# Fire attention's bias stage: the Relu of a round is taken ahead of the copies of that round's queries and keys

## The chip, the cores and the metric

The kernel runs on one core of a Trainium2 chip. Its engines work side by side, each through its own list of instructions in order: TensorE (PE, with its weight loads shown apart as PEld), VectorE (DVE), ScalarE (ACT), GpSimd (POOL) and SyncE (SP), which here only issues DMAs. They wait for one another through semaphores. The metric is the device time of one execution in microseconds (us), the median of several; lower is better.

## The reference, cut to what matters

The program is a chain of layers on a residual of 2048 tokens by 128 channels, held as 8 batches of 256 tokens. The change touches one layer, attention with a Fire bias, 16 heads of 8 channels:

```
rel  = log(|c * (i - j)| + 1);  pos_norm = log(|c * max(i, threshold)| + 1) + 1e-6
nd   = rel / pos_norm                              # [256, 256]
h    = relu(nd[..., None] * w1 + b1)               # [256, 256, 32]
bias = einsum('tsw,wh->hts', h, w2) + b2           # [16, 256, 256], -inf above the diagonal
att  = softmax(q @ k.T * scale + bias);  y = (att @ v) @ Wproj + bproj
```

The bias doesn't depend on the batch. It is computed once, and q, k and v once for each of the 8 batches.

## The kernel before, in words

All layers run one after the other, each in blocks of code that end in a barrier of all engines. Ahead of Fire attention run two mixtures of experts, a recurrence and a six-layer local transformer; behind it a second local transformer. Fire attention has three blocks. The first loads and prepares `rel` and `pn` (the distances and their reciprocal norms). The second, the bias stage, is the one that is changed. The third computes the scores, the softmax and the output for each batch; it is called the score stage below.

The bias stage has 8 rounds. Round r does two unrelated things: it computes the bias for 32 key positions, and the queries, keys and values of batch r. Its steps, by engine:

- TensorE `project(r)`: four matmuls for queries and keys (the line that the profile calls L1474), then four for values (L1478). Then `biases(r)` (L1488): it waits for the round's Relu (`hd_`) and runs 32 small matmuls in rounds 0 to 3, and 16 in rounds 4 to 7, where half of the keys lie above the diagonal.
- VectorE: `distances(r + 1)` (L1422, eight products into `nd`), then `take_values(r)` (L1435), then `take_bias(r)` (L1428), which waits for the matmuls of `biases(r)`. `distances(0)` stands ahead of the loop. `distances(r)` waits until the Relu of round r - 2 has read its half of `nd`.
- ScalarE: `take_queries(r)` copies the queries (L1457) and the keys (L1461) out of PSUM once `project(r)` has made them; `hidden(r)` (L1452) is one Relu over 128 x 2048 elements, from `nd` to `hb`. It waits for `distances(r)` and for the matmuls of `biases(r - 2)`, which read the same half of `hb`.
- GpSimd: `spread_keys(r)` (L1500) waits for the copy of the keys; then `forget_future(r)` (L1507) waits for `take_bias(r)`.

`nd`, `hb`, `kT` and the PSUM banks of each step are double, by r % 2. Nothing but these lists of instructions and the waits sets the order.

Of the kernel before, what the change touches and what calls it, by code (L numbers as in the profile page):

```python
# [1315 lines left out]
def fire_attention_phase(nc, res, d, M, XN):  # L1316
# [8 lines left out]
    with ExitStack() as ctx:  # L1325
# [43 lines left out]
        with nc.Block() as block:  # L1369
            @block.sync  # L1370
            def _(sp):
                for dst, src in ((sc[:, 0:2], d["fa_sc"].to_broadcast([P, 2])), (rel[:, :], d["c_rel"]), (pn[:, :], d["c_pos"]),
                                 (wb[:, :], d["fa_wb"]), (wqkv[:, :], d["fa_wqkv"]), (bqk[:, :], d["fa_bqk"]),
                                 (bv[:, :], d["fa_bv"].to_broadcast([P, P])), (b2[:, :], d["fa_b2"].to_broadcast([P, NH])),
                                 (hmask[:, :], d["c_hmask"]), (wp[:, :], d["fa_wp"])):
                    sp.dma_start(dst, src).then_inc(ld, 16)
                sp.wait_ge(zd, 1)
                for g in range(4):
                    sp.dma_start(w2[g * BW:(g + 1) * BW, g * NH:(g + 1) * NH], d["fa_w2"]).then_inc(ld, 16)
                sp.wait_ge(ld, 16 * 14)  # L1380
# [33 lines left out]
        with nc.Block() as block:  # L1414
# [31 lines left out]
            @block.scalar  # L1446
            def _(act):
                def hidden(r):
                    act.wait_ge(ndd, r + 1)
                    if r >= 2:  # L1450
                        act.wait_ge(bp, r - 1)
                    nc.scalar.activation(hb[:, r % 2, :, :], nd[:, r % 2, :, :], ACT.Relu, scale=wb[:, 0:1],  # L1452
                                         bias=wb[:, 1:2]).then_inc(hd_, 1)

                def take_queries(b):
                    act.wait_ge(qkp, b + 1)
                    nc.scalar.activation(qT[:, b, :], bank[4 + b % 2][:, 0:T], ACT.Identity, bias=sc[:, 3:4],  # L1457
                                         scale=SCALE).then_inc(qE, 1)
                    if b >= 2:
                        act.wait_ge(kzd, b - 1)  # L1460
                    nc.scalar.activation(kT[:, b % 2, :], bank[4 + b % 2][:, T:2 * T], ACT.Identity, bias=bqk[:, 1:2]).then_inc(kE, 1)  # L1461
                for r in range(8):
                    take_queries(r)
                    hidden(r)

            @block.tensor
            def _(pe):
# [67 lines left out]
        with nc.Block() as block:  # L1535
            @block.gpsimd
            def _(pool):
                def slot(n):
                    q = at(n, SIM)
                    if q is not None:  # L1540
                        _, _, _, _, nh, nk = info(q)
                        s = S[:, q % 8, :].rearrange("p (h k) -> p h k", h=nh)
                        pool.wait_ge(mxd, q + 1)
                        nc.gpsimd.tensor_tensor(s, s, mx[:, q % 8, 0:nh].unsqueeze(2).to_broadcast([P, nh, nk]),
                                                ALU.subtract).then_inc(subd, 1)
                stream(slot)

            @block.tensor
            def _(pe):
# [8 lines left out]
                def scores(q):  # L1558
                    if q:
                        pe.wait_ge(addd, q)  # L1560
                    for r in range(GR):
                        b, _, t, a, nh, nk = info(q + r)
                        rows = slice(32 * r, 32 * r + 32)
                        nc.tensor.matmul(bank[r][:, :].rearrange("p (h k) -> p h k", h=nh),
                                         qT[rows, b, t * P:(t + 1) * P], kz[rows, b, a:a + nh, 0:nk],
                                         start=True, stop=True).then_inc(simd, 1)
# [89 lines left out]
            def _(dve):  # L1656
                def add_bias(q):
                    _, r, t, a, nh, nk = info(q)
                    s = S[:, q % 8, :].rearrange("p (h k) -> p h k", h=nh)
                    dve.wait_ge(simd, q + 1)  # L1660
                    if q >= 8:
                        dve.wait_ge(ptT, q - 7)
                    nc.vector.tensor_tensor(s, bank[r][:, :].rearrange("p (h k) -> p h k", h=nh),
                                            bias[t][:, 4 * r + a:4 * r + a + nh, 0:nk], ALU.add).then_inc(addd, 1)
# [186 lines left out]
```

## Time and profile before

| | us |
|---|---|
| median of 3 runs (4397.21, 4402.37, 4403.71) | 4402.37 |
| the profiled execution | 4395.94 |
| its span, first to last instruction | 4394.2 |
| the bias stage, 2316.79 to about 2391.9 of the span | 75 |
| the score stage behind it, from 2392.2 | about 300 |

Over the whole span TensorE is busy for 88%, VectorE for 78%, ScalarE for 72% and GpSimd for 61%, at a mean granted TensorE clock of 0.936 of full speed (1.0 is 2.4 GHz, 0.5 is 1.2 GHz). In the bias stage it is TensorE for 56.9 of 75.2 us, VectorE for 45.5, ScalarE for 22.5 and GpSimd for 24.2, at a mean clock of 0.64, with hardly any DMA. So the averages of the whole say little of this stage; it has to be read by its own timeline.

In a timeline a row is a run of instructions of one line on one engine: start, time from the first to the last end, what it is, and in brackets how long the engine had been idle before it and what ended that.

### The profile page before, as it was taken

To read this page: it belongs to the slowest core of one execution; us is meant where nothing else is said; L and a number is where in the kernel's file an instruction comes from. 1 tells how busy PE (TensorE), PEld (TensorE's weight loads), DVE (VectorE), ACT (ScalarE), POOL (GpSimd) and SP (SyncE) were. 2 spreads that over 40 slices of the span, in tenths; PEclk is the share of its full clock that TensorE was granted. 3 is DMA by queue.
4 is the path that set the end of the run, shared out by engine and by line. 5 is a ranking of instruction groups with operands and counts; after the bars stand their busy time and mean duration, and the time that the engine had idled before them with its cause. 6 is when DMAs were issued, how large, how long until landed. Compare 5 with 4: busy or idle time off the path is not lost. (4 is left out here: it accounts for less than half of the span.)

```text
span 4394.2 us, 163943 instructions
## 1 busy us (share of the span) xinstructions
PE 3849.0 (88%) x64208; PEld 2781.2 (63%) x64208; DVE 3408.9 (78%) x6643; ACT 3185.7 (72%) x10371; POOL 2692.8 (61%) x2514
## 2 busy tenths in 40 slices
PE   7966968999999999999966665899999999999996
PEld 3423427777777777777745443777777777777773
DVE  1122129999999999999945444999999999999994
ACT  3443437888888888888843433788888888888884
POOL 1110128777777777777723332778777777877772
PEclk8987989999999999999976776999999999999997
DMA  1101113333333333333310000333333333333331
GB/s 58 58 15 44 58 47 103 114 103 117 102 117 104 104 117 105 115 96 109 117 33 7 1 1 33 103 118 103 116 100 117 103 107 114 104 117 96 109 117 39
DMA packets 549312, 377.94 MB, mean 86 GB/s; under 512 B 32576, under 2 KB 533056, under 8 KB 546240
## 3 DMA queue, kind: packets, MB, share of 16 engines
q1 hardware_dynamic: 548560, 367.57, 27.8%
q8 instruction: 514, 8.42, 0.8%
q14 instruction: 238, 1.95, 0.1%
HBM read 265.37 MB, written 102.11 MB: 84 GB/s over the span
## 5 line engine op out<-in xcount | busy, mean ns | idle before, releaser
L1266 POOL TENSOR_TENSOR lt_t<-lt_t 128x512 f32<-128x512 f32 x768 | 973.4, 1289 | 566.9 <-DVE lt_t L1100 566.9
L1002 ACT ACTIVATE lt_pb<-lt_pb,lt_mx 128x64 f32<-128x64 f32 x3072 | 1023.7, 346 | 0.0
L1272 POOL TENSOR_TENSOR lt_t<-lt_t,lt_rn 128x512 f32<-128x512 f32 x768 | 810.9, 1076 | 116.9 <-DVE lt_rn L1128 115.6
L49 PE MATMUL ps<-lt_wh,lt_xh 128*128 128x512 f32 (+1 forms) x1536 | 580.2, 378 | 150.5 <-DVE lt_t L1100 88.7
L1002 ACT ACTIVATION_READ_ACCUMULATOR lt_pb<-lt_pb,lt_mx 128x1 f32 x3072 | 611.5, 199 | 0.0
L984 ACT ACTIVATE lt_qkT<-ps 128x512 f32<-128x512 f32 x768 | 459.0, 598 | 196.5 <-PE ps L804 196.1
L1111 DVE TENSOR_REDUCE lt_ss<-lt_sq 128x8 f32<-128x512 f32 x768 | 518.3, 675 | 14.1 <-ACT lt_sq L979 10.1
L1100 DVE TENSOR_TENSOR lt_t<-ps,lt_tab 128x512 f32<-128x512 f32 x768 | 522.3, 680 | 2.9
L1106 DVE TENSOR_TENSOR lt_t<-ps,lt_tab 128x512 f32<-128x512 f32 x768 | 520.9, 678 | 2.1 <-PE ps L804 0.8
L51 PE MATMUL ps<-lt_wh,lt_xl 128*128 128x512 f32 (+1 forms) x1536 | 522.4, 340 | 0.0
L50 PE MATMUL ps<-lt_wl,lt_xh 128*128 128x512 f32 (+1 forms) x1536 | 521.0, 339 | 0.0
L804 PE MATMUL ps<-ident,lt_t 128*128 128x128 f32 x3072 | 482.1, 280 | 35.1 <-ACT lt_qkT L984 25.4
L979 ACT ACTIVATE lt_sq<-ps 128x512 f32<-128x512 f32 x768 | 452.5, 589 | 69.2 <-PE ps L51 68.6
L49 PEld LDWEIGHTS ps<-lt_wh,lt_xh 128*128 128x128 f32 x1536 | 289.6, 189 | 269.5 <-issue 151.5
L804 PEld LDWEIGHTS ps<-ident,lt_t 128*128 128x128 f32 x3072 | 355.4, 141 | 160.2 <-issue 106.7
L862 PEld LDWEIGHTS ps<-lt_pT,lt_vw 64*64 64x64 f32 x24576 | 398.0, 135 | 88.3 <-issue 88.0
L862 PE MATMUL ps<-lt_pT,lt_vw 64*64 64x32 f32 x24576 | 440.0, 221 | 3.1 <-issue 3.1
L1278 POOL TENSOR_TENSOR lt_pb<-lt_pb,lt_rd 128x512 f32<-128x512 f32 x384 | 400.6, 1043 | 29.9 <-DVE lt_rd L1145 26.9
L876 PE MATMUL ps<-lt_oT,lt_wo 128*128 128x256 f32 x1536 | 405.0, 386 | 1.4 <-ACT lt_oT L1014 1.4
L372 POOL TENSOR_TENSOR M<-M,moe_tmp 128x512 f32<-128x512 f32 x64 | 80.9, 1264 | 511.2 <-DVE moe_tmp L354 511.2
L354 DVE SCALAR_TENSOR_TENSOR moe_tmp<-ps,moe_bb,moe_cbc 128x512 f32<-128x512 f32 x64 | 48.0, 750 | 421.4 <-PE ps L306 421.4
L832 PEld LDWEIGHTS ps<-lt_qkT 64*32 64x32 f32 x24576 | 270.1, 105 | 136.2 <-issue 133.7
(200 smaller groups left out, 7823.6 us busy)
## 6 DMA issues: line engine op xcount, KB each, us to landing
lt_vw<-v_scratch SPq DMA_DIRECT2D x768, 256.0 KB, 3.8
v_scratch<-lt_vv SPq DMA_DIRECT2D x384, 256.0 KB, 2.1
lt_wraw<-in_lt_wqkv SPq DMA_DIRECT2D x56, 384.0 KB, 5.7
moe_cbc<-comb_scratch SPq DMA_DIRECT2D x16, 1024.0 KB, 6.5
moe_w<-in_moe_w SPq DMA_DIRECT2D x32, 256.0 KB, 2.8
lt_wo<-in_lt_wo SPq DMA_DIRECT2D x48, 128.0 KB, 3.7
lt_w<-in_lt_w SPq DMA_DIRECT2D x12, 341.0 KB, 4.5
lt_w<-in_lt_w SPq DMA_DIRECT2D x12, 192.0 KB, 4.1
```

Source lines behind the costliest of these rows:

```text
L49: nc.tensor.matmul(out, lh, rh, start=start, stop=False)
L50: nc.tensor.matmul(out, lh, rl, start=False, stop=False)
L51: return nc.tensor.matmul(out, ll, rh, start=False, stop=stop)
L804: ins = nc.tensor.transpose(TB[:, q * P:(q + 1) * P], t1[:, u[1] % 2, t, q * P:(q + 1) * P], ident[:, :])
L862: ins = nc.tensor.matmul(OR[r][64 * e:64 * e + 64, t * P + w * WIN:t * P + w * WIN + WIN], vw[h, k, 4 * t + w, e * DH:(e + 1) * DH], pT[h, ...
L984: nc.scalar.activation(qkT[:, u[1] % 2, :, WIN + t * P:WIN + (t + 1) * P], TB.rearrange("p (a n) -> p a n", a=4), ACT.Copy).then_inc(tE[t], 1)
L1002: ins = nc.scalar.activation(p, p, ACT.Exp, bias=mx[:, par, c:c + 1], accum_out=sm[:, par, c:c + 1])
L1100: nc.vector.tensor_tensor(o4, a4[:, :, :, ::-1, :], s4, ALU.mult).then_inc(rotd[t], 1)
L1106: nc.vector.tensor_tensor(t1[:, u[1] % 2, t, :].rearrange("p (w h c) -> p w h c", w=2, c=DH), A[t][:, :].rearrange("p (w h c) -> p w h c", ...
L1111: nc.vector.tensor_reduce(ss[:, u[1] % 2, 8 * t:8 * t + 8], sq[:, t, :].rearrange("p (h c) -> p h c", c=DH), AX.X, ALU.add).then_inc(ssd[t ...
L1266: nc.gpsimd.tensor_tensor(o, o, t2[:, t, :], ALU.add).then_inc(padd[t], 1)
L1272: nc.gpsimd.tensor_tensor(o, o, rn[:, u[1] % 2, 8 * t:8 * t + 8].unsqueeze(2).to_broadcast([P, 8, DH]), ALU.mult).then_inc(qkd[t], 1)
```

## The change

ScalarE's loop calls `hidden(r)` before `take_queries(r)`:

```
                 for r in range(8):
+                    hidden(r)
                     take_queries(r)
-                    hidden(r)
```

No wait, buffer or instruction is added or removed, and no other engine's list changes. In ScalarE's list, at the entry to the stage, L1452 is the Relu, L1457 the copy of the queries, L1461 that of the keys:

```order
 L1369 UNCONDITIONAL_BRANCH
 L1446 UNCONDITIONAL_BRANCH
+L1452 ACTIVATE fa_hb<-fa_nd,fa_wb 128x2048
 L1457 ACTIVATE fa_qT<-ps,fa_sc 128x256
 L1461 ACTIVATE fa_kT<-ps,fa_bqk 128x256
```

The Relu of round 0 now stands first. From there the three instructions alternate as they did, so that behind the copies of round r comes the Relu of round r + 1, where it was that of round r. At the end of the stage, ahead of the branches into the score stage:

```order
 L1457 ACTIVATE fa_qT<-ps,fa_sc 128x256
 L1461 ACTIVATE fa_kT<-ps,fa_bqk 128x256
-L1452 ACTIVATE fa_hb<-fa_nd,fa_wb 128x2048
 L1414 UNCONDITIONAL_BRANCH
 L1618 UNCONDITIONAL_BRANCH
```

The copies of round 7 are now ScalarE's last work in the stage, and the Relu of round 7 stands ahead of them.

## Rows read from the trace of the kernel before

**Rows 1.** Waits from 2312 to 2392: who waited for whom, total, times, longest

```profile
ACT fa_qT L1457 <- PE ps L1474: 51.2, 8, 9.0
DVE fa_bias L1428 <- PE ps L1488: 26.8, 8, 6.3
PE ps L1488 <- ACT fa_hb L1452: 16.7, 8, 2.3
```

**Rows 2.** Timeline of rounds 0 and 1: start, us, engine, line, [idle before, releaser]

```profile
2316.79 5.45 DVE L1422 TENSOR_TENSOR fa_nd<-fa_rel,fa_pn 128x256 f32<-128x256 f32 x16 [0.30 <-PEq L1369]
...
2319.60 2.09 ACT L1452 ACTIVATE fa_hb<-fa_nd,fa_wb 128x2048 f32<-128x2048 f32 x1
...
2321.75 7.09 PE L1488 MATMUL ps<-fa_w,fa_hb 128*128 128x64 f32 x32 [2.06 <-ACT fa_hb L1452]
...
2328.63 2.02 PE L1474 MATMUL ps<-XN,fa_wqkv 128*128 128x256 f32 x4
2328.88 1.29 DVE L1428 TENSOR_TENSOR fa_bias<-ps,fa_b 128x512 f32<-128x512 f32 x2 [6.29 <-PE ps L1488]
...
2330.08 5.04 DVE L1422 TENSOR_TENSOR fa_nd<-fa_rel,fa_pn 128x256 f32<-128x256 f32 x8
...
2330.44 1.06 PE L1478 MATMUL ps<-fa_wqkv,XN 128*128 128x128 f32 x4
2330.69 0.47 ACT L1457 ACTIVATE fa_qT<-ps,fa_sc 128x256 f32<-128x256 f32 x1 [8.99 <-PE ps L1474]
2331.06 0.47 ACT L1461 ACTIVATE fa_kT<-ps,fa_bqk 128x256 f32<-128x256 f32 x1
2331.42 2.09 ACT L1452 ACTIVATE fa_hb<-fa_nd,fa_wb 128x2048 f32<-128x2048 f32 x1
2331.61 1.89 POOL L1500 TENSOR_TENSOR fa_kz<-fa_kT,fa_hmask 128x1024 f32<-128x1024 f32 x1 [0.49 <-ACT fa_kT L1461]
...
2333.56 5.65 PE L1488 MATMUL ps<-fa_w,fa_hb 128*128 128x64 f32 x32 [2.05 <-ACT fa_hb L1452]
2335.05 0.41 DVE L1435 TENSOR_TENSOR fa_vv<-ps,fa_bv 128x256 f32<-128x256 f32 x1
...
2339.00 2.02 PE L1474 MATMUL ps<-XN,fa_wqkv 128*128 128x256 f32 x4
```

**Rows 3.** The same timeline in rounds 4 to 7

```profile
2368.18 0.69 DVE L1428 TENSOR_TENSOR fa_bias<-ps,fa_b 128x512 f32<-128x512 f32 x1 [1.23 <-PE ps L1488]
2368.79 4.97 DVE L1422 TENSOR_TENSOR fa_nd<-fa_rel,fa_pn 128x256 f32<-128x256 f32 x8
...
2372.86 3.67 PE L1488 MATMUL ps<-fa_w,fa_hb 128*128 128x64 f32 x16 [2.05 <-ACT fa_hb L1452]
...
2376.33 2.02 PE L1474 MATMUL ps<-XN,fa_wqkv 128*128 128x256 f32 x4
...
2381.26 2.15 PE L1488 MATMUL ps<-fa_w,fa_hb 128*128 128x64 f32 x16 [2.06 <-ACT fa_hb L1452]
...
2383.20 2.02 PE L1474 MATMUL ps<-XN,fa_wqkv 128*128 128x256 f32 x4
...
2390.37 0.69 DVE L1428 TENSOR_TENSOR fa_bias<-ps,fa_b 128x512 f32<-128x512 f32 x1 [3.83 <-PE ps L1488]
```

**Rows 4.** Busy us by engine (instructions), then granted clock, in stretches of 1 us

```profile
2324.00:2325.00 1.00, 1.00 (x6) 1.00 (x6) 0.00 (x0) 0.00 (x0) 0.00 (x0) 0.50 0.00 0
...
2332.00:2333.00 1.00, 0.00 (x0) 0.00 (x0) 1.00 (x1) 1.00 (x1) 1.00 (x1) 1.00 0.00 0
...
2334.00:2335.00 1.00, 1.00 (x11) 1.00 (x10) 1.00 (x4) 0.00 (x0) 0.00 (x0) 1.00 0.06 16
...
2336.00:2337.00 1.00, 1.00 (x7) 1.00 (x7) 0.00 (x0) 0.00 (x0) 0.00 (x0) 0.50 0.00 0
```

**Rows 5.** TensorE's timeline of the score stage: score matmuls of four groups

```profile
2438.87 1.14 PE L1564 MATMUL ps<-fa_kz,fa_qT 32*128 32x512 f32 x8
2452.64 2.09 PE L1564 MATMUL ps<-fa_kz,fa_qT 32*128 32x512 f32 x8
2465.88 1.14 PE L1564 MATMUL ps<-fa_kz,fa_qT 32*128 32x512 f32 x8
2476.49 1.14 PE L1564 MATMUL ps<-fa_kz,fa_qT 32*128 32x512 f32 x8
```

## The prediction

> **What bounds the kernel now.** I read the waits of the stage first, then its timeline round by round, then the granted clock in short stretches, and last the stage behind it. The list of waits shows three large ones [rows 1]. ScalarE waits 51.2 us for the projections and VectorE 26.8 us for the bias matmuls; both are idle engines behind a slower one. The third is the slower one's own: TensorE waits for the Relu in all 8 rounds, 16.7 us together, 2.1 each. The timeline shows why [rows 2]. In round 1 TensorE projects from 2328.63 to 2331.50 (2330.44 + 1.06). ScalarE, idle for 8.99 us by then, copies queries and keys from 2330.69 and only then starts the Relu, at 2331.42. TensorE stands still until 2333.56. But the Relu's input is VectorE's distances, and those of the next round end at 2330.08 + 5.04 = 2335.12, in the first third of the bias matmuls of round 1, which last until 2339.00. So the Relu of round 2 lacks nothing from 2335.12 on except its turn behind the copies of round 2, and those wait for a projection that TensorE starts at 2339.00.
>
> **The change part by part.**
>
> Nothing is added or removed, and only ScalarE's list moves: 8 Relus of 2.09 us pass ahead of 16 copies of 0.47 us. No DMA is issued in the stage, and no queue of SP is passed.
>
> *Round 0.* The Relu needs the first eight of sixteen products. These take half of 5.45 us, so they are done near 2316.79 + 2.72 = 2319.5, and before it began at 2319.60 [rows 2]. The bias matmuls of round 0 start where they did; this round gains nothing. The copies of round 0 now end about 2322.5 instead of 2319.7. What waits for them is the spreading of the keys on GpSimd and TensorE's projection of round 2, both far off.
>
> *Rounds 1 to 7, the wait.* With the Relu early, TensorE goes from the values' matmuls straight into the bias matmuls. Round 1 now takes 2333.56 - 2328.63 = 4.93 us from projection to bias matmuls, of which 2.87 are work; 2.06 us go. Seven times that is 14.4 us.
>
> *Is the Relu early enough?* From VectorE's side the Relu of round r + 1 can start when the distances end, and its buffer is then free, since the distances themselves start behind the bias of round r - 1. It ends 2.09 us later: 2335.1 + 2.1 = 2337.2 for round 2, ahead of any projection of round 2 that TensorE could have finished (it can't end before about 2338.3, below). Yes for rounds 2 to 6, with less and less to spare.
>
> *What is late next: VectorE.* Back to back its round is bias, distances, values: 2335.05 + 0.41 - 2328.88 = 6.58 us with two bias tiles [rows 2]. With one tile the bias step is half as long, 2368.79 - 2368.18 = 0.61 us to the next start [rows 3] in place of 1.20, so 5.9 to 6.0 us; I take 5.9. TensorE's round without its wait is 2.87 plus the bias matmuls. Those depend on the clock. At the low level (0.50, which is 1.2 GHz) 32 of them take 2328.63 - 2321.75 = 6.88 us [rows 2], and 16 take 2376.33 - 2372.86 = 3.47 [rows 3]. At the high level (1.00, 2.4 GHz) 16 take 2383.20 - 2381.26 = 1.94 [rows 3]. So TensorE's round is 9.8 or 6.7 us in rounds 1 to 3, and 6.3 or 4.8 in rounds 4 to 7: with the high clock VectorE is the bound.
>
> *The clock in round 1.* Nothing on TensorE differs until 2331.5, and at 2332 to 2335 the clock is high, though the first 1.5 us of it are idle; it is low again from 2336 [rows 4]. Now the 32 bias matmuls start at 2331.5 and can run through in 2 x 1.94 = 3.9 us, where they took 2339.00 - 2333.56 = 5.44. That is another 1.5 us.
>
> *The walk through the rounds.* I keep 3.9 for round 1 and for the others the durations that they had (5.6, 5.8, 2.8, 3.5, 1.9, 2.2 us in rounds 2 to 7, from rows like those shown), so the clock's mix stays as it was:
> - Round 1: bias matmuls 2331.5 to 2335.4; VectorE takes the bias at 2335.5 (before: 2339.25).
> - Round 2: projected by 2338.3, bias matmuls to 2343.9, taken at 2344.1.
> - Round 3: projected by 2346.7, done 2352.5, taken 2352.7.
> - Round 4: projected by 2355.4, done 2358.2. VectorE's distances run 2353.9 to 2358.9, so the bias is taken at 2359.3: VectorE now sets the pace.
> - Rounds 5 and 6: taken 5.9 us after each other, 2365.2 and 2371.1.
> - Round 7: distances until 2370.7, Relu until 2372.8, matmuls until 2375.1, taken at 2375.3.
>
> Before, this last one was at 2390.37 [rows 3]. The stage is shorter by 15.1 us. The barrier and the stages behind I count as unchanged, so the sum is 15.1.
>
> *The bounds of it.* If all rounds after 0 ran at the low clock, the 14.4 us would stand against 1.4 + 1.3 + 1.1 + 0.7 + 0 + 1.5 + 1.5 = 7.5 us of slower bias matmuls: 6.9 gained. If they all ran at the high clock, VectorE alone would set the time: biases taken at 2328.88, then three rounds of 6.58, one of 6.58 (the two tiles of round 3), two of 5.9, and a last Relu and matmuls: 2367.0 for round 6, and about 2371 to 2372.5 for round 7. That is 18 to 19 us gained.
>
> *The clock against a page.* The row shows TensorE fully busy at 2324 to 2325 at clock 0.50, in the third microsecond of a run of bias matmuls that stays at 0.50 to its end, and clock 1.00 at 2332 to 2333 with TensorE idle [rows 4]. The Trainium skill, TensorE: Matmul & The Clock Gate, section Part 1: The HAM clock gate, says that the throttle is the resting state and sustained matmul activity releases it, as a kernel without long gaps stays fast. By that page the stage without its waits would run at the high level, and the time would be that of the first rival below; by this trace being busy with these small matmuls isn't enough.
>
> *A block between VectorE and GpSimd.* The eight distances take 5.04 us in round 1 but half of 5.45 for eight in round 0: 2.3 us more, when GpSimd spreads the keys for 1.89 us from 2331.61 [rows 2]. If spreading moved away from the distances, VectorE's round would shrink by up to 2.3 us. By the walk it doesn't: where VectorE sets the pace, the keys' copy ends about 3.1 us behind one set of distances, and the next set runs from 1.1 or 1.6 us behind it for five. So I count nothing. The Trainium skill, SBUF — State Buffer, section Who interferes with whom, calls this port an exclusive lock held for a whole instruction; the trace agrees.
>
> **The rivals.**
>
> *A: the clock goes high.* TensorE's idle share falls from a quarter to little, and if that lifts the clock for most of the stage, 18 to 19 us go: 4383 to 4384. Against it: the busy stretch at 0.50.
>
> *B: the clock stays low.* The high stretches came with projections near, and their phase may be lost. Then 7 to 10 us go: 4392 to 4395. For it: the same busy stretch.
>
> *C: the score stage pays more.* This one ends slower. That stage repeats groups of 13.77, 13.24 and 10.61 us, 12.54 on average (2476.49 - 2438.87 over three), with short score matmuls (1.14) in some and long (2.09) in others: it has locked into a pattern with the clock [rows 5]. It now starts 15 us earlier against the clock's own changes and could lock otherwise. If all its 24 groups (three for each of 8 batches) took 13.77, that would be 24 x 1.23 = 29.5 us more, net 4417. It is slower than before by over 0.2% once the mean group passes 12.54 + (15.1 + 8.8) / 24 = 13.5 us. Against it: two of the three kinds of group already sit near that length and the pattern repeats evenly. It could as well turn out shorter.
>
> *D: the Relu isn't early.* If its distances came late, TensorE would wait as before, and the time would be 4402. The 2335.12 against 2339.00 speaks against it.
>
> **How the numbers follow.** Main forecast 0.60, A 0.13, B 0.15, C 0.05, D 0.03, and 0.04 for a score stage that locks into a shorter pattern. The profiled execution took 4395.94 us, which would become 4380.8. It is 6.4 us under the median of the runs shown, so by the median I forecast 4402.4 - 15.1 = 4387.3, and take 4387. Runs scatter by 6.5 us (4397.2 to 4403.7), a median of them by 2 or 3. The range goes from A less that scatter (4379) to B with it (4398). A measurement can tell about 0.2%, 8.8 us: faster means under 4393.6. All of A, nearly all of the main case, the short pattern and a third of B give 0.80; D, the rest of B and a little of the main case 0.15; C 0.05.
>
> **What would show it.** In the profile after, TensorE's wait for the Relu falls from 16.7 us to about 2 for round 0 and at most 2 more in rounds 5 to 7. The first bias matmuls still start near 2321.7. VectorE's wait for them falls from 26.8 us to about 12, and the stage lasts about 60 us. The score stage's groups stay at 12.5 us on average. I am wrong if TensorE still waits 2 us in each round, if the bias matmuls sum to far more than before, or if the score stage's length changes by over 5 us.

## The result and the profile after

| | before | after |
|---|---|---|
| median, first comparison (6 runs each) | 4400.57 us | 4380.27 us |
| median, second comparison (17 and 6 runs) | 4400.91 us | 4385.84 us |
| bias stage, first projection to first score matmul | 75.5, 79.8, 76.2 us | 58.5, 56.6 us |
| score stage, first to last group of score matmuls | 285.8, 285.4, 285.2 us | 285.2, 286.2 us |
| from the first score matmul to the end of the span | 2001.9, 1998.2, 2001.0 us | 2004.5, 1997.1 us |

The ratio of after to before is 0.9955, 95% interval 0.9942 to 0.9967, in the first comparison and 0.9965 (0.9953 to 0.9977) in the second: 20 and 15 us. The rows below the medians come from profiled executions, three of before and two of after (the first of each, then e10 and e11, and e1, from the experiments).

The first profiled executions took 4395.94 and 4384.40 us. Their spans are 11.6 us apart, though the stage alone lost 16.9: the rest of the kernel took 5.3 us more in that pair (2.8 ahead of the stage, 2.5 behind it). Over all five, the span is 17.6 us shorter on average and the stage 19.6. Behind the stage nothing was gained: 2000.4 us on average before, 2000.8 after. The waits of the changed stage, as in [rows 1] (total, times, longest):

```profile
ACT fa_hb L1452 <- DVE fa_nd L1422: 25.5, 7, 5.2
...
DVE fa_bias L1428 <- PE ps L1488: 10.5, 3, 6.3
...
ACT fa_qT L1457 <- PE ps L1474: 7.7, 2, 6.3
PE ps L1488 <- ACT fa_hb L1452: 6.9, 4, 2.8
```

ScalarE now waits for VectorE's distances where it waited for TensorE's projection. VectorE waits for bias matmuls in 3 rounds of 8, so in the other five it sets its own pace. TensorE's wait for the Relu is 6.9 us in 4 rounds, from 16.7 in 8. The timeline of rounds 1 and 2, and then of round 5:

```profile
2331.43 2.02 PE L1474 MATMUL ps<-XN,fa_wqkv 128*128 128x256 f32 x4
2331.68 1.29 DVE L1428 TENSOR_TENSOR fa_bias<-ps,fa_b 128x512 f32<-128x512 f32 x2 [6.29 <-PE ps L1488]
...
2333.24 1.04 PE L1478 MATMUL ps<-fa_wqkv,XN 128*128 128x128 f32 x4
...
2334.10 3.70 PE L1488 MATMUL ps<-fa_w,fa_hb 128*128 128x64 f32 x32
2334.41 2.15 POOL L1500 TENSOR_TENSOR fa_kz<-fa_kT,fa_hmask 128x1024 f32<-128x1024 f32 x1 [0.20 <-ACT fa_kT L1461]
...
2337.64 1.08 PE L1474 MATMUL ps<-XN,fa_wqkv 128*128 128x256 f32 x4
...
2337.89 2.10 ACT L1452 ACTIVATE fa_hb<-fa_nd,fa_wb 128x2048 f32<-128x2048 f32 x1 [3.56 <-DVE fa_nd L1422]
2338.11 1.27 DVE L1428 TENSOR_TENSOR fa_bias<-ps,fa_b 128x512 f32<-128x512 f32 x2
...
2340.03 3.79 PE L1488 MATMUL ps<-fa_w,fa_hb 128*128 128x64 f32 x32 [0.87 <-ACT fa_hb L1452]
...
2357.36 0.61 PE L1478 MATMUL ps<-fa_wqkv,XN 128*128 128x128 f32 x4
...
2360.73 3.06 PE L1488 MATMUL ps<-fa_w,fa_hb 128*128 128x64 f32 x16 [2.75 <-ACT fa_hb L1452]
```

In round 1 the bias matmuls follow the values' matmuls without a gap and take 3.70 us, where they took 5.65 [rows 2]. The projection of round 2 takes 1.08 us instead of 2.02: it too runs at the high clock. The Relu of round 2 then comes late by 0.87 us, since VectorE's distances end only then; in round 5 it is 2.75.

One line of busy time over the stage (length, then PE, PEld, DVE, ACT, POOL busy, granted clock) for the changed kernel:

```profile
2319.59:2378.12 58.53, 49.58 (x256) 46.15 (x257) 44.97 (x84) 22.68 (x24) 22.59 (x16) 0.67 0.00 1
```

and for the kernel before:

```profile
2316.79:2392.26 75.47, 56.88 (x257) 51.59 (x257) 45.50 (x84) 22.54 (x24) 24.18 (x16) 0.64 0.00 1
```

The same 256 matmuls keep TensorE busy for 49.6 us instead of 56.9, and its idle time is 8.9 instead of 18.6. So 7.3 of the 16.9 us are faster matmuls and 9.6 are idle time. The high clock isn't there throughout, even without waits. In rounds 5 to 7 of the changed kernel:

```profile
2362.00:2376.00 14.00, 13.92 (x57) 12.90 (x56) 9.53 (x16) 5.64 (x6) 6.71 (x5) 0.50 0.00 1
```

TensorE is busy for 13.92 of these 14.00 us, and its clock is at the low level all the while.

### The profile page after: what moved, and what is told of

It reads as the page before. It is cut to its first block and busy times, and to the rows that moved or that the text cites. A ratio compares the mean times of both kernels' runs of the same rounds, so it can differ in the third digit from the quotient of the medians.

```text
span 4382.6 us, 163943 instructions
## 1 busy us (share of the span) xinstructions
PE 3848.6 (88%) x64208; PEld 2780.6 (63%) x64208; DVE 3410.3 (78%) x6643; ACT 3187.3 (73%) x10371; POOL 2694.2 (61%) x2514
## 5 line engine op out<-in xcount | busy, mean ns | idle before, releaser
L1111 DVE TENSOR_REDUCE lt_ss<-lt_sq 128x8 f32<-128x512 f32 x768 | 518.9, 676 | 14.3 <-ACT lt_sq L979 9.7
```

Source lines behind the costliest of these rows:

```text
L1111: nc.vector.tensor_reduce(ss[:, u[1] % 2, 8 * t:8 * t + 8], sq[:, t, :].rearrange("p (h c) -> p h c", c=DH), AX.X, ALU.add).then_inc(ssd[t ...
```

## The experiments

All numbers are of the stage in us (the clock aside), one profiled execution each. "Waits" are TensorE's for the Relu, "bias" the busy time of its bias matmuls, "clock" the granted one as a share of 2.4 GHz.

| kernel | stage | PE busy | PE idle | waits | bias | clock |
|---|---|---|---|---|---|---|
| before | 75.5 | 56.9 | 18.6 | 16.7 | 35.5 | 0.64 |
| e10, before again | 79.8 | 60.7 | 19.1 | 17.2 | 39.9 | 0.59 |
| e11, before again | 76.2 | 57.5 | 18.7 | 16.8 | 36.3 | 0.61 |
| after | 58.5 | 49.6 | 8.9 | 6.9 | 32.6 | 0.67 |
| e1, after again | 56.6 | 47.3 | 9.3 | 7.4 | 30.5 | 0.71 |
| e2, Relu between the copies | 72.8 | 56.5 | 16.3 | 14.4 | 35.4 | 0.64 |
| e3, after, Relu twice | 68.6 | 51.5 | 17.1 | 15.2 | 34.9 | 0.67 |
| e4, before, Relu twice | 98.9 | 64.6 | 34.2 | 32.3 | 43.1 | 0.50 |
| e5, after, keys direct | 49.5 | 42.8 | 6.8 | 4.7 | 28.4 | 0.78 |
| e6, before, keys direct | 94.1 | 63.8 | 30.3 | 28.3 | 42.5 | 0.57 |
| e7, Relu first in rounds 0 to 3 | 65.4 | 50.8 | 14.7 | 12.7 | 32.4 | 0.68 |
| e8, Relu first in rounds 4 to 7 | 72.6 | 56.3 | 16.3 | 14.3 | 38.2 | 0.62 |
| e12, the same again | 67.7 | 52.8 | 14.9 | 12.9 | 34.5 | 0.68 |
| e9, before, filled waits | 62.5 | 51.6 | 10.9 | 9.0 | 26.2 | 0.83 |

**After again (e1), no edit.**

> The changed kernel once more. In its first profile the bias stage (first projection to first score matmul) took 58.5 us, before 75.5, while the medians differ by 20.3 us. My theory (all the gain lies in the bias stage: TensorE's wait for the Relu is gone, then VectorE or the clock sets the pace) expects a stage of 56 to 61 us again and a whole that is 14 to 19 us under before. The rival, that 3 us or more come from the stages behind, expects 20 us or more again in the whole with a stage that is only 17 shorter.

The stage was 56.6 us and the whole 15.1 us under before (10 to 21 by the interval). My theory's numbers came. The three profiles of before average 77.2 us in the stage and the two of after 57.6, so the stage alone can carry the 20 us of the first comparison as well; the stages behind gave nothing (the last row of the result's table). The two comparisons don't tell 15 from 20.

**The Relu between the two copies (e2, on the kernel before).**

```
+                def take_keys(b):        # the copy of the keys, until now the second half of take_queries
...
                 for r in range(8):
                     take_queries(r)      # now the queries only
                     hidden(r)
+                    take_keys(r)
```

> Before, with the Relu between the copy of the queries and that of the keys. My theory: the Relu still stands behind the projection, and only the 0.37 us from one copy's start to the next go, in each of 8 rounds: TensorE's wait for the Relu falls from 16.7 to about 13.8 us, the stage from 75.5 to about 72.5, the whole by 3. The rival, that the gain came from the later copy of the keys (GpSimd then spreads them away from VectorE's distances), expects most of the 17 us here.

The stage took 72.8 us, the waits 14.4, the whole 0.9988 of before (0.9977 to 0.9998), 4 us less: as my theory had it. Round 1 shows both theories at once:

```profile
2336.74 3.27 DVE L1422 TENSOR_TENSOR fa_nd<-fa_rel,fa_pn 128x256 f32<-128x256 f32 x8
...
2337.35 0.47 ACT L1457 ACTIVATE fa_qT<-ps,fa_sc 128x256 f32<-128x256 f32 x1 [8.63 <-PE ps L1477]
2337.72 2.08 ACT L1452 ACTIVATE fa_hb<-fa_nd,fa_wb 128x2048 f32<-128x2048 f32 x1
...
2339.86 7.09 PE L1491 MATMUL ps<-fa_w,fa_hb 128*128 128x64 f32 x32 [1.69 <-ACT fa_hb L1452]
...
2340.25 1.89 POOL L1503 TENSOR_TENSOR fa_kz<-fa_kT,fa_hmask 128x1024 f32<-128x1024 f32 x1 [2.17 <-ACT fa_kT L1463]
```

The keys' spreading does leave the distances, which fall from 5.0 to 3.27 us, and TensorE gains nothing from it (its bias matmuls take 35.4 us in the stage, before 35.5): with this order VectorE has time to spare. What counts is the Relu's place relative to the projection.

**The Relu twice (e3 on after, e4 on before).**

```
+                    if r:
+                        act.wait_ge(hd_, r)
+                    nc.scalar.activation(hx[:, :, :], nd[:, r % 2, :, :], ACT.Relu, ...)   # hx is read by nothing
                     nc.scalar.activation(hb[:, r % 2, :, :], nd[:, r % 2, :, :], ACT.Relu, ...)
```

> The changed kernel with a second Relu of the same size ahead of each, into a tile that nothing reads. It puts the Relu off by 2.1 us. My theory: this costs its full 2.1 us in rounds 0 and 7 and only 0 to 2 us in each of the others, where it fits beside TensorE's matmuls: 4 to 10 us in the stage. The rival, that the Relu is still wholly on the path and only the copies were taken off, expects 8 x 2.1 = 16.8 us.

> The kernel before with the same second Relu. Both theories expect 2.1 us in each of 8 rounds, 16 to 18 us in the stage, since there the Relu stands between the projection and the bias matmuls.

On the kernel before, the waits grew by 15.6 us, about as expected, and the stage by 23.4 (19 to 23 against the three profiles of before), more than either theory said: the clock was at the low level, 0.50, throughout. On the changed kernel the waits grew by 8 us and the stage by 10 to 12, a little above the range of 4 to 10. So the Relu is partly on the path after the change, behind VectorE's distances. TensorE's timeline of e3 shows the two kinds of round:

```profile
2342.44 0.83 PE L1482 MATMUL ps<-fa_wqkv,XN 128*128 128x128 f32 x4
2343.10 3.68 PE L1492 MATMUL ps<-fa_w,fa_hb 128*128 128x64 f32 x32
2346.62 1.08 PE L1478 MATMUL ps<-XN,fa_wqkv 128*128 128x256 f32 x4
2347.54 0.61 PE L1482 MATMUL ps<-fa_wqkv,XN 128*128 128x128 f32 x4
2351.21 5.38 PE L1492 MATMUL ps<-fa_w,fa_hb 128*128 128x64 f32 x32 [3.07 <-ACT fa_hb L1456]
```

In one round the doubled Relu is hidden wholly, in the next TensorE waits 3.07 us for it. The whole of e3 was 4387.3 us (8 runs, from 4381 to 4401), which is 1.4 and 7 us over the medians of after in two other comparisons, less than the 10 to 12 us of its stage. Its profiled execution, 4386.8 us, was a typical one, and the stage started 2.2 and 3.3 us earlier in it than in those of after; the rest of the kernel scatters by several us. How much the doubled Relu costs the whole isn't settled.

**Keys written straight by ScalarE (e5 on after, e6 on before).** Four copies, each with its own mask, take the place of one copy and GpSimd's product.

```
-                    nc.scalar.activation(kT[:, b % 2, :], bank[4 + b % 2][:, T:2 * T], ACT.Identity, bias=bqk[:, 1:2]).then_inc(kE, 1)
+                    for g in range(GR):
+                        ins = nc.scalar.activation(kz[:, b, g, :], bank[4 + b % 2][:, T:2 * T], ACT.Identity,
+                                                   bias=kb[:, g:g + 1], scale=hmask[:, g:g + 1])   # kb = hmask * bqk[:, 1]
+                    ins.then_inc(kE, 1)
...
-                    spread_keys(r)      # GpSimd's product
```

> The changed kernel, with the keys written by ScalarE straight to their spread form (four scaled copies of 256 instead of one, no GpSimd product). My theory: GpSimd no longer stops VectorE, eight distances take 2.7 to 2.9 us instead of 5.0, VectorE's round falls from 6.5 to about 4.4, and TensorE becomes the bound. Its waits of 0.9, 1.3, 2.8 us in rounds 2, 3 and 5 go and the stage falls by 3 to 7 us, less if the clock is lower. The rival, that VectorE doesn't set the pace after the change, expects no gain from it (within 1 us).

> The same edit on the kernel before. My theory: VectorE had slack there, so its shorter distances bring nothing; the four copies stand ahead of the Relu and put it off by 3 x 0.37 = 1.1 us in each round, so the stage is 8 to 9 us longer. If VectorE had been a bound before as well, the stage would be shorter.

One edit, opposite signs. On the changed kernel the stage fell to 49.5 us, 7 to 9 less where 3 to 7 were expected, and the whole to 4373.8 us beside e1's 4385.8 in the same comparison: 0.9938 of before (0.9924 to 0.9952). On the kernel before the stage rose to 94.1 us and the whole to 4418.5: 1.0035 (1.0022 to 1.0048). Round 3 of e5:

```profile
2345.76 3.27 DVE L1423 TENSOR_TENSOR fa_nd<-fa_rel,fa_pn 128x256 f32<-128x256 f32 x8
...
2346.33 3.79 PE L1490 MATMUL ps<-fa_w,fa_hb 128*128 128x64 f32 x32 [0.45 <-ACT fa_hb L1453]
2346.54 1.92 ACT L1461 ACTIVATE fa_kz<-ps,fa_kb,fa_hmask 128x256 f32<-128x256 f32 x4
2348.96 0.41 DVE L1436 TENSOR_TENSOR fa_vv<-ps,fa_bv 128x256 f32<-128x256 f32 x1
```

The distances take 3.27 us, not 5.0 (2.7 to 2.9 were expected), and the four copies stand behind that round's Relu. VectorE now waits for the bias matmuls in 6 rounds of 8, 12.9 us together, where it waited in 3: it isn't the late one any more. But TensorE's idle time fell by only 2.1 and 2.5 us against the two profiles of after. The rest, 6.8 and 4.5 us, is faster matmuls, at a clock of 0.78; that is why the gain was over the range. On the kernel before the same four copies stand between projection and Relu:

```profile
2341.16 1.93 ACT L1461 ACTIVATE fa_kz<-ps,fa_kb,fa_hmask 128x256 f32<-128x256 f32 x4
2342.96 2.11 ACT L1453 ACTIVATE fa_hb<-fa_nd,fa_wb 128x2048 f32<-128x2048 f32 x1
...
2345.12 7.09 PE L1490 MATMUL ps<-fa_w,fa_hb 128*128 128x64 f32 x32 [3.73 <-ACT fa_hb L1453]
```

The wait is 3.73 us instead of 2.06, and the stage grew by 18.6 (14 to 19 against the three profiles of before) where 8 to 9 were expected. The waits grew by 11.6, since the four copies hold the Relu up by 1.80 us from their start (2341.16 to 2342.96) where the one held it up by 0.36 [rows 2]: 1.44 more per round, not 1.1. The bias matmuls grew by 7.0 (2.6 to 7.0 against the three): their 42.5 us are near the 43.1 that they take in e4 at the low level. In e4 and e6 a longer wait cost more than itself.

**The Relu first in some rounds only (e7; e8 and e12).**

```
                 for r in range(8):
+                    if r < 4:            # e7; r >= 4 in e8 and e12
+                        hidden(r)
+                        take_queries(r)
+                    else:
                         take_queries(r)
                         hidden(r)
```

> The Relu is ahead of the copies in rounds 0 to 3 only. In the profile of the changed kernel the projection of round 4 came 10.9 us earlier than before, and the rounds from there gave 6.1 more. My theory: the rounds gain on their own, so this stage is 9 to 12 us shorter than before. The rival, that the gain hangs on TensorE's unbroken work through the stage (the clock), expects well under 9.

> The Relu is ahead of the copies in rounds 4 to 7 only. My theory: 4 x 2.06 = 8.2 us of waits go, less what VectorE's round of 5.9 us gives back, so the stage is 5 to 8 us shorter than before, and this and the run of rounds 0 to 3 add up to about 17. The rival of the clock expects a sum that misses 17 by more than 4.

> The Relu first in rounds 4 to 7 only, a second look. If the clock's chance made the first look's rounds 1 to 3 slow, they may now sum to 31 to 35 us, while the changed rounds 4 to 7 again take about 6 us less than before's 32.1. If it was the edit, rounds 1 to 3 take 34.9 again.

> The kernel before once more, for its stage by rounds. In the run with the Relu first in rounds 4 to 7 only, the untouched rounds 1 to 3 took 11.3 to 11.8 us each, where the profile of before has 10.4 to 10.7. If that is the clock's chance, looks at one kernel differ: rounds 1 to 3 sum to anything from 31.6 to 35.5 us, the stage is 75 to 81 us, and TensorE's waits for the Relu stay at 16.5 us each time. If it was the edit, this look repeats 31.6 and 75.5.

> The same once more: a third look at the stage of the kernel before, with the same two readings. By my theory the waits are the same and only the bias matmuls differ, by the granted clock.

Against the first profile of before e7 gained 10.1 us, as expected. e8 gained 2.9 and missed, and the sum of 13 spoke for the rival. Three more profiles (e10, e11, e12) show why. Rounds 1 to 3, which e8 and e12 don't touch, took 34.9 us in e8 and 31.7 in e12, and 31.6, 34.9 and 30.4 in the three profiles of the kernel before: the clock's chance, at nearly the same waits (16.7, 17.2 and 16.8 us in the stage). Taken part by part, rounds 1 to 3 are 20.5 us in e7 beside a mean of 32.3 before, and rounds 4 to 7 are 25.8 and 24.2 beside a mean of 33.1. That is 11.8 + 8.1 = 19.9 us, and the whole change, mean against mean, is 19.6. Within the spread of the profiles, which is over 4 us for one kernel, the rounds add up.

**TensorE's waits filled on the kernel before (e9).**

```
+                def filler(b):
+                    if b >= 2:
+                        pe.wait_ge(be, b - 1)
+                    for w in range(2):
+                        nc.tensor.matmul(bank[2 * (b % 2) + 1][:, w * T:(w + 1) * T], wqkv[:, w * P:(w + 1) * P], x, ...)
                 for r in range(8):
                     project(r)
+                    filler(r)
                     biases(r)
```

> The kernel before, with two more projections per round (four matmul rows of 256 columns, into a PSUM bank that the round's bias matmuls overwrite) in the place where TensorE waits for the Relu. At the low clock they take 1.8 of the 2.06 us, so they add nothing to the path, and the Relu stays where it was. If TensorE's idle time was also what held the clock down, the bias matmuls of the stage fall from 35.5 us towards 24 and the stage to 64 to 71 us. If only the wait mattered (the clock doesn't answer to it), the stage stays at 72 to 78 us.

This leaves ScalarE's order alone and only adds work to TensorE, whose results are overwritten. The stage fell to 62.5 us and the whole to 4383.9: 0.9959 of before (0.9944 to 0.9974), as much as the change itself. The forecast for the stage was 64 to 71, so it gained a little more than expected. Round 0 shows it at once; its bias matmuls take 7.09 us in the kernel before and in the changed one:

```profile
2321.78 1.91 PE L1497 MATMUL ps<-XN,fa_wqkv 128*128 128x256 f32 x4
2324.04 3.79 PE L1488 MATMUL ps<-fa_w,fa_hb 128*128 128x64 f32 x32 [0.35 <-ACT fa_hb L1452]
```

TensorE in rounds 2 and 3:

```profile
2339.04 1.91 PE L1497 MATMUL ps<-XN,fa_wqkv 128*128 128x256 f32 x4
2341.30 3.79 PE L1488 MATMUL ps<-fa_w,fa_hb 128*128 128x64 f32 x32 [0.35 <-ACT fa_hb L1452]
2344.93 1.08 PE L1474 MATMUL ps<-XN,fa_wqkv 128*128 128x256 f32 x4
2345.84 0.61 PE L1478 MATMUL ps<-fa_wqkv,XN 128*128 128x128 f32 x4
2346.29 1.03 PE L1497 MATMUL ps<-XN,fa_wqkv 128*128 128x256 f32 x4
2348.92 5.10 PE L1488 MATMUL ps<-fa_w,fa_hb 128*128 128x64 f32 x32 [1.60 <-ACT fa_hb L1452]
```

The 32 bias matmuls take 3.79 us in one round and 5.10 in the next, where at the low clock they take 7.09. The mean clock is 0.83. The kernel's own matmuls, line by line, sum to 45.0 us instead of 61.5 (the mean of the three profiles of before). So in the kernel before the low clock cost about as much as the waits themselves, 16.9 us.

What lifts the clock is only in part shown. e9 fills the gap and adds projections at the same time. In the kernel before, the clock rises six times in the stage, each time within 0.4 us of the end of a round's values' matmuls; and the changed kernel worked for 14 us almost without a gap at 0.50 (above). Over all 14 profiles, longer waits go with slower bias matmuls: 26 to 33 us at waits under 10, 32 to 40 between 12 and 18, 42 to 43 above 28. But where the waits are longer, the projections are also further apart. A filler of the small bias matmuls would tell the two apart; it wasn't run.

## Why the prediction was right, and where its terms were off

The forecast was 4387 us, 15.1 less than before, in a range from 4379 to 4398. The first comparison gave 4380.3, near the lower end, and the second 4385.8. The profiled execution took 4384.4 us, forecast 4380.8. The mechanism was right; that the size came out so near is partly luck, as two terms were off in opposite directions.

- *The Relu is early enough, and TensorE's wait goes.* Right for round 1, and in part for the others: e2 and the changed kernel's profile show that its place behind the projection had held it. Round 0 gained nothing (11.84 us to the next projection, before and after).
- *Round 1.* 3.9 us were forecast for its bias matmuls at the high clock, from their start to the next matmul's, 3.54 were measured (3.70 to the last end); the biases were taken 6.43 us after those of round 0, forecast 6.6.
- *VectorE is late next.* Right in kind: its biases of rounds 4 to 6 were taken 5.8 us apart, forecast 5.9, and in e5, with shorter distances, it waits for TensorE again. But it came two rounds sooner than the walk had it. I let TensorE's waits end at "about 2 for round 0 and at most 2 more"; they are 6.9 and 7.4 us, in the first profile with 0.87 in round 2, 1.26 in round 3 and 2.75 in round 5. Of the 14.4 us of waits only 9.8 went.
- *The step that failed is the walk's "for the others the durations that they had".* Without its waits TensorE got the high clock more often. Its busy time fell by 7.3 us in the pair of profiles, 9.9 between the means (58.4 to 48.4), not by the 1.5 of the forecast; part of that is the projections, which I had kept at 2.87 us each. In round 2 they took 1.52 us (2337.64 to 2339.16), and that is why the Relu came late there: by the prediction's own numbers TensorE's round at the high clock was 6.7 us in rounds 1 to 3, no shorter than VectorE's 6.6. The two errors have opposite signs: fewer waits gone, faster matmuls. They leave 16.9 (19.6 between the means) against 15.1.
- *The clock against a page.* The Trainium skill, TensorE: Matmul & The Clock Gate, section Part 1: The HAM clock gate, lets sustained work release the throttle, and I set that aside because a fully busy stretch was at 0.50 [rows 4]. e9 agrees with the page in kind: with the waits filled the clock was 0.83. The 14 us of nearly gapless work at 0.50 in the changed kernel don't, and there the measurement decides.
- *Rival A.* Its time (18 to 19 us) fits the means better than mine did; its picture, the high level for most of the stage, doesn't: the mean clock is 0.67 and 0.71, from 0.59 to 0.64 before.
- *Rival B* would have had slower matmuls than before; they are faster. *Rival C* is out as far as these runs go: in all 14 profiles the score stage takes 284.8 to 286.7 us, a mean of 12.4 us a group, though it starts up to 49 us apart. *Rival D* falls with the waits.
- *The block between VectorE and GpSimd* stayed inside the distances, as said: 4.96 us for eight, 3.27 where GpSimd's product keeps out (e2, e5).
- Open: whether the whole gained 15 or 20 us, as profiles of one kernel's stage differ by 4 us, nearly all of it in the clock (TensorE busy for 56.9 and 60.7 us, waits of 16.7 and 17.2); and what lifts the clock in such a stage.

## What to carry to other kernels

When an engine with cheap work stands between two pieces of TensorE's work, put first the operation whose input is already there, and check which engine is late next before counting the whole wait. Where TensorE's clock is seen to move in the stage, don't keep the durations of its matmuls as they were, and forecast them as a range between the two levels: here the faster matmuls gave as much again as the waits that went (9.9 us, and 9.7 of idle time, between the means), while in e4 and e6 the slower ones added 3 to 8 us to 11 to 16 of longer waits. And compare a short stage over several profiles, since the clock alone moved this one by 4 us.

## What the runs showed that I had not expected

- Adding 32 useless matmuls (16 in the code, which the trace shows as two each) to the kernel before made it 16 us faster (4383.9 beside 4399.7).
- The best version is e5, 4373.8 us, 27 under before: a fourfold copy on ScalarE in place of a GpSimd product frees VectorE of 10.6 us over the stage (its distances fall from 35.2 to 24.6 us), but only once the Relu no longer waits behind that copy.
- With the Relu doubled on the kernel before, TensorE was at the low clock, 0.50, for the whole stage, in the one execution profiled (4419.8 us).
- The changed kernel's TensorE worked through its last rounds almost without a gap, 13.92 us busy in 14.00, and stayed at the low clock.
